# An AdaLN attention and mixture-of-experts block: one-time work between the first batches' operations, written-out orders, and one split f32r product for projection and centred output

## The reference

```python
mod = (silu(c) @ wmod).reshape(16, 6, 1, -1)      # sa, ca, ga, sb, cb, gb
ga, gb = [(2 * (g >= 0) - 1) * maximum(abs(g), 0.25) for g in (ga, gb)]
h = layernorm(x) * (1 + ca) + sa
q, k, v = h @ Wq.T + bq, h @ Wk.T + bk, h @ Wv.T + bv     # 16 heads of 8
q = softmax(q, over the 8 channels of a head); k = softmax(k, over the 512 tokens)
state = k.T @ v                                    # per head, 8 x 8
o = layernorm(q @ state) * ln_g + ln_b
x = x + ga * (o @ Wo.T + bo)
h = layernorm(x) * (1 + cb) + sb
y = sum over the 2 best of 8 experts of p_e * (gelu(h @ w_in[e] + b_in[e]) @ w_out[e] + b_out[e])
x = x + gb * y
```

## Time and profile before

| what | us |
|---|---|
| median of 3 runs | 392.83 (391.58 to 394.48) |
| the profiled execution, its own time | 392.8 |
| its span, first to last instruction | 391.1 |
| PE busy / PEld busy | 362.9 / 327.3 |
| DVE / ACT / POOL busy | 282.5 / 278.5 / 216.8 |
| mean granted TensorE clock | 0.965 |

### The profile page before, as it was taken

One profiled execution on the slowest core, in us unless ns is written; L12 is line 12 of the kernel. 1 busy time (PEld: TensorE's weight loads), 2 busy tenths in 40 slices (PEclk: granted clock), 3 DMA queues, 4 the chain that ended last, 5 costly groups with the idle time before them and its releaser, 6 DMA issues.

```text
span 391.1 us, 8091 instructions
## 1 busy us (share of the span) xinstructions
PE 362.9 (93%) x2502; PEld 327.3 (84%) x2502; DVE 282.5 (72%) x1060; ACT 278.5 (71%) x502; POOL 216.8 (55%) x221
## 2 busy tenths in 40 slices
PE   3657789999999999999999999999999999999995
PEld 3446679889999999899899999898998999988875
DVE  2665586787777888878877778788788787786432
ACT  3333679688787969696887879696969878675740
POOL 2315447373938466483838384664837383754543
PEclk9966579999999999999999999999999999999999
DMA  5570051240706071321606070605224150605061
GB/s 182 151 297 2 0 173 73 80 193 24 247 5 242 29 225 47 157 115 41 231 33 241 3 244 27 240 32 168 106 104 169 38 208 3 217 28 216 32 227 41
DMA packets 18817, 47.83 MB, mean 122 GB/s; under 512 B 2571, under 2 KB 6102, under 8 KB 18518
## 3 DMA queue, kind: packets, MB, share of 16 engines
q1 hardware_dynamic: 18576, 46.90, 33.3%
q10 hardware_dynamic: 198, 0.41, 0.3%
HBM read 42.82 MB, written 4.48 MB: 121 GB/s over the span
## 4 chain that ended last, share of the span: by engine, by line
PE 66%; DVE 9%; issue 6%; DMA 6%; POOL 5%; SPq 4%; ACT 2%; POOLq 0%; DVEq 0%; ACTq 0%
PE pY L684 19%; PE pH L672 6%; PE pH L674 6%; PE pH L673 6%; PE pB L661 4%; PE pQV L641 4%; PE pC L629 4%; PE pC L648 3%; POOL v L355 2%; DVE qn L876 2%; DMA gate_bc<-route_scratch 2%; DMA gates<-gate_scratch 2%; SPq L236 2%; DVE elg_cut L934 2%; PE pA L588 2%
## 5 line engine op out<-in xcount | busy, mean ns | idle before, releaser
L684 PE MATMUL pY<-wout,v 128*128 128x128 f32 x1024 | 128.7, 277 | 1.0 <-DVE v L958 0.7
L684 PEld LDWEIGHTS pY<-wout,v 128*128 128x128 f32 x1024 | 121.7, 193 | 2.2 <-DVE v L958 1.1
L502 ACT ACTIVATE u<-pH,cols 128x512 f32<-128x512 f32 x128 | 86.4, 689 | 49.5 <-PE pH L674 42.8
L344 POOL TENSOR_TENSOR rstd_o<-ve_o,neg_half 128x4 f32<-128x4 f32 x16 | 22.0, 1376 | 104.3 <-DVE ve_o L895 104.3
L958 DVE TENSOR_TENSOR v<-u,gate_bc 128x512 f32<-128x512 f32 x80 | 68.6, 860 | 7.0 <-DMA gate_bc<-route_scratch 3.7
L355 POOL TENSOR_TENSOR v<-u,gate_bc 128x512 f32<-128x512 f32 x48 | 63.7, 1329 | 9.0 <-DMA gate_bc<-route_scratch 9.0
L672 PE MATMUL pH<-h_hi,win_hi 128*128 128x512 f32 x128 | 54.9, 429 | 1.4 <-ACT u L502 1.4
L673 PE MATMUL pH<-h_hi,win_lo 128*128 128x512 f32 x128 | 50.6, 395 | 0.0
L674 PE MATMUL pH<-h_lo,win_hi 128*128 128x512 f32 x128 | 50.5, 394 | 0.0
L349 POOL TENSOR_TENSOR h_lo<-h,h_hi 128x512 fp32r<-128x512 f32 x16 | 22.5, 1405 | 20.2 <-ACT h_hi L440 20.2
L452 ACT ACTIVATE xn<-x_all,nmr,rstd 128x128 f32<-128x128 f32 x64 | 26.2, 482 | 4.5 <-POOL nmr L372 4.5
(11 more groups left out here) (151 smaller groups left out, 781.5 us busy)
## 6 DMA issues: line engine op xcount, KB each, us to landing
gate_bc<-route_scratch SPq DMA_DIRECT2D x64, 512.0 KB, 5.7
x_all<-in_L_attn_x SPq DMA_DIRECT2D x16, 256.0 KB, 6.9
out<-x_all SPq DMA_DIRECT2D x16, 256.0 KB, 2.0
gates<-gate_scratch SPq DMA_DIRECT2D x1, 2048.0 KB, 7.1
gb_bc<-gb_scratch SPq DMA_DIRECT2D x1, 1024.0 KB, 4.6
route_scratch<-gateT SPq DMA_DIRECT2D x64, 4.0 KB
win<-in_L_ffn_w_in SPq DMA_DIRECT2D x1, 512.0 KB, 5.6
wout<-in_L_ffn_w_out SPq DMA_DIRECT2D x1, 512.0 KB, 6.9
```

What stands on the lines that cost most here:

```text
L344: pool.tensor_tensor(rstd_o[:, :], ve_o[:, :], neg_half[:, :], ALU.pow).then_inc(s["rstdo_ready"], 1)
L502: act.activation(u[:, e % U, :], pH[:, e % 2, :], ACT.Gelu_apprx_tanh, bias=cols[:, e:e + 1]).then_inc(s["gelu_done"], 1)
L684: i = mm(pY[:, t * P:(t + 1) * P], v[:, e % U, t * P:(t + 1) * P], wout[:, e, :], start=False, stop=(e == NE - 1), skip_group_check=True)
```

## The change

**One product in place of two.** `attend_centred` and `attend_project` become `attend`: per chunk three f32r matmuls of 256 columns, 12 in all, into `pQV` (before, the projection went to `pC`). `qT` and `sw` become rounded high parts, written by ACT as before, and DVE makes the low parts (`q_low`, `sw_low`). `sq` and `residual1` now read `pQV`, so that `qv(n)` waits for `x1_ready` of batch n - 1, and `state(n)` no longer does.

**One-time work** is cut into functions that stand among the first batches' operations; waits on it move to the operations of batch 0 that use it. The gates are broadcast in two parts, two batches first. Two of the weight loads move to ACT's queue; each load of x signals one of four semaphores.

**Orders.** PE, DVE, ACT, POOL and SP get written-out orders for the first and last batches, and a new `step` between. Cut to its core:

```diff
 PE
-            def attend_centred(n):
-                pe.wait_ge(s["sw_ready"], n + 1)
-                pe.wait_ge(s["qT_ready"], n + 1)
-                for t in range(T):
-                    i = mm(pQT[:, t * P:(t + 1) * P], qT[:, t * P:(t + 1) * P], sw[:, 1, :], start=True, stop=True)
...
+            def attend(n):
+                pe.wait_ge(s["swlow_ready"], n + 1)
+                pe.wait_ge(s["qlow_ready"], n + 1)
+                for t in range(T):
+                    o = pQV[:, t, :, :].rearrange("p a c -> p (a c)")
+                    ts = slice(t * P, (t + 1) * P)
+                    mm(o, qT_hi[:, ts], sw_hi[:, :], start=True, stop=False)
+                    mm(o, qT_hi[:, ts], sw_lo[:, :], start=False, stop=False)
+                    i = mm(o, qT_lo[:, ts], sw_hi[:, :], start=False, stop=True)
+                i.then_inc(s["att_done"], 1)
             def qv(n):
-                w(pe, "sq_ready", n)
+                w(pe, "x1_ready", T * n)
...
+            turn_weights()
+            modulation()
+            hT(0)
+            gain_centred()
+            residual_gates()
+            kT(0)
...
+            gate_turn(15)
+            hidden(14, 6)
+            hidden(14, 7)
+            combine(14, 4)
 DVE
+            def q_low(n):
+                dve.wait_ge(s["qT_ready"], n + 1)
+                w(dve, "att_done", n)
+                dve.tensor_tensor(qT_lo[:, :], pQT, qT_hi[:, :].bitcast(F32), ALU.subtract).then_inc(s["qlow_ready"], 1)
+
+            def sw_low(n):
+                dve.wait_ge(s["sw_ready"], n + 1)
+                w(dve, "att_done", n)
+                dve.scalar_tensor_tensor(out=sw_lo[:, :], in0=pSW, scalar=kinv[:, 0:1], in1=sw_hi[:, :].bitcast(F32),
+                                         op0=ALU.mult, op1=ALU.subtract).then_inc(s["swlow_ready"], 1)
 SP
-                sp.dma_start(gates[:, :, :, :].rearrange("p b w c -> p (b w c)"),
...
+            def spread_first_gates():
+                sp.wait_ge(s["gates_stored"], DMA)
+                sp.dma_start(gates[:, 0:FIRST, :, :].rearrange("p b w c -> p (b w c)"),
```

More of the change, by code:

```diff
@@ L388, in step @@
[L388 to L402 removed]
+                    h_low(b + 4)
@@ L733, in step @@
[L733 to L746 removed]
+                q_turn(b + 2)
+                logits(b + 1)
```

1116 lines of the change are left out of this document (860 added, 256 removed).

## The result

The changed kernel took 401.21 us (median of four runs, 398.88 to 403.47), the kernel before 393.54 beside it: a ratio of 1.0201, 95% interval 1.0122 to 1.028. It is slower by 2%, where 382.8 was forecast and 374.5 to 391 was the range. Its profiled execution took 402.42 us, with a span of 400.7.

The account below looks back on a forecast made before the run. PE's work was taken to fill the loop, 20.93 of 21.44 us a batch, with whole microseconds to gain at start and end. Sum: 392.8 - 4.1 (loop) - 2.2 (start) - 3.7 (end) = 382.8 us; range 374.5 to 391.

Parts of the forecast that it names:

- SP's queue: In the start: the larger part of the gates' broadcast delays only x of batch 3, which nobody needs for 10 us.
- The low parts on DVE: In the loop: q_low 0.69 and sw_low 0.42 us; DVE's busy time from 17.06 to 18.2 us a batch, which fits.
- PE's side of the product: In the loop: 1.42 us for 1.78, with 0.24 given back by f32/f32r changes; PE's work from 20.93 to 20.81.
- The circle: In the loop: from out_var through DVE's work to route and ACT's squares, 20.9 us, as long as PE's work.
- the signs that it named: In the loop: period 21.1 us, out_var's group waiting over 1 us a batch for ACT's squares, attend for no low part.
- the prediction's own signs of being wrong: attend starting late for qT_lo or sw_lo, L958's mean rising beyond 0.95, or the first combine standing after 63 us.
- Twelve periods: Loop between the start and the last batches: 0.34 us saved a period, times 12, 4.1 us; upper bound 7.5.
- The start: First batches: kT(0) at 13.7, gate_turn(0) at 50, first combine at 60.6; 2.2 us saved together, bounds 0 and 7.
- its upper bound: In the start: 7 us saved if PE keeps its full clock.
- The end: Last three batches: 1.5 us of idle time left of 5.2, 3.7 us saved, bounds 1 to 5.
- The rival of slower meetings: In the loop: more DVE operations meet POOL's, 1.1 us a meeting; priced at one and a half a batch, 400 us; chance 0.10.
- the dense loop of 20.9: Loop without PE waits: PE's work 20.81 us; as a rival with a warm start, period 20.85, time 376.7 us, chance 0.20.

Follow-up runs that it names:

- e1: The changed kernel with the loads of x of batches 4 to 10 issued one step earlier in SP's order: 393.37 us, ratio 1.0015.
- e4: e1 with one f32 product of 256 columns in place of the split one, and no low parts: 385.73 us, ratio 0.9779.
- e9: The changed kernel, late loads of x kept, with one f32 product of 256 columns and no low parts: 393.72 us, ratio 1.0019.
- e5: The kernel before with only the loads of x from batch 4 on issued one step later: 524.87 us, ratio 1.3335.
- e11: e1 with both low parts still made by DVE and waited for by PE, but the product in f32 without them: 397.72 us, ratio 1.0107.
- e8: e1 with POOL adding the constant row to one chunk of x of four, a shorter operation: 396.15 us, ratio 1.0069.

## Why the prediction was wrong

**The step that failed: SP's queue.** The prediction says that "the larger part behind it has only x of batch 3 to delay, which nobody needs for 10 us". That came true (batch 3's x led by 15.3 us), but it looked at the start alone, and the sum has no term for the loads of the loop. The new order takes every batch's statistics one step earlier against its load, so that the lead fell from about 18 us to as little as 4.7, where the transfer took 8.8. By e1, e4 and e9 this cost 7 to 9 us in the medians and ratios, and e5, which puts the same order of load and statistics into the kernel before, lost 132 us. It is as large as the measured loss; the other losses and gains of the change cancel (e1, 1.0015).

**The low parts on DVE, priced in the loop alone.** PE's side of the product was sized well: "That is 0.36 saved" and 0.24 given back leave PE's work at 20.81, and in e1 the period of 21.22 less its stop of 0.38 is 20.84. The pieces were off: the product takes 1.51 and not 1.42, and the changes give back less. "The circle is 20.9 us ... so I take a period of 21.1" came true (21.2), with the signs that it named: `out_var` waits 1.10 us a batch for the squares, and `attend` waits for no low part in the loop. Without the low parts the stop is gone and the period is 20.87 (e4), with them and the f32 product it is 21.2 (e11). What the sum lacks is their cost ahead of the loop: of the 9.2 us between the profiled spans of e1 and e4, 5.2 lie in the first six intervals (138.5 us for 133.3). There `attend(2)` does start late for `sw_lo`, by 1.45 us, and `attend(1)` in the start for `qT_lo`, by 0.98, one of the prediction's own signs of being wrong.

**Twelve periods.** "times the 12 periods between the start and the last batches" took the loop's pace for intervals that do not have it. In e1, without late loads, the windows of the first four intervals are
```profile
57.39:150.63 93.24, 87.88 (x627) 78.96 (x625) 84.36 (x272) 75.37 (x130) 59.12 (x53) 1.00 0.37 130
```
and in e4
```profile
56.21:147.32 91.11, 88.88 (x608) 79.73 (x608) 79.94 (x264) 75.28 (x129) 58.36 (x53) 1.00 0.39 136
```
In e1 they take 93.2 us for 4 x 21.1 = 84.4; before, 86.0. PE works 87.9 us in them for 85.3, as work of later batches is pulled ahead (627 instructions for 621, though each batch has four fewer); the last batches have that much less. The rest is idle time, 5.4 us for 0.7: waits for `sw_lo`, `qn`, `yg` and `s2T`. In e4 it is 2.2.

**The start** came out near, by compensation and by its clock: `kT(0)` at 15.85 for 13.7, since the second x landed only at 11.02 and DVE stood before it; the first gates' part landed at 23.69 for "before 20"; `gate_turn(0)` at 49.20 for 50, `combine(0, 0)` at 60.35 for 60.6. The start's stage gives 0.6 us after, 1.7 in e1 and 2.9 in e4, for 2.2, all three with a better clock than the profile before (0.83 to 0.89 for 0.60). At 0.63 and 0.66 the new start is longer than the old one, by 2.8 us in e9 and 1.8 in e11. So at a clock near that of before the new start gave nothing; the sum had put a warmer start only into its upper bound. Whether the new order has a part in the clock is not shown.

**The end** seems right and is not: from batch 14's bias on it is 3.4 us shorter in e1 and e4, for 3.7, but of these 2.7 are work that the new order does ahead of that mark (PE is busy 25.61 us behind it before, 22.93 and 22.92 there). The sum had 3.7 us less of idle time in the last three batches, from 5.2. From batch 13's bias to the span's end PE is idle 6.6 us before, with the 4.5 behind its last matmul, which leaves 2.1 to save from. In e1 and e4 it is 5.6 and 5.5: 1.0 saved. The changed kernel saves none, with waits of 0.39 and 0.54 us for DVE at `moe_bias(15)` and at the combine behind it.

**The rival of slower meetings** got a tenth of the chances, with "only placed anew" against it. DVE's busy time rose by 29.7 us, not by 16 x 1.11 = 17.8. The weighing's mean did not rise, it fell from 860 to 796 ns; the meetings went to operations that I had not counted, because they are small: `echosen`, 192 ns on average before, takes 633, `gateT_r` 408 for 227, the first norm's `ve` 318 for 170. What these meetings cost can't be told from e8.

With the late loads and the low parts taken out, e4 has the dense loop of 20.9 that the working describes. Its span is 9.4 us under that of before, where the sum had 10.0, and that the two agree is in part luck: e4's profiled run is its fastest, at the highest clock (383.46 us at a mean of 0.991; 386.55 at 0.982). The nine intervals of the loop give 4.2, the first four take 5.1 back, and start and last batches together give 10.3, of which 3.5 are work moved into the first four, for the 5.9 forecast.

## What to carry to other kernels

When an order is rewritten, list every transfer's lead in the steady loop, from its issue to its first use, and set it against its landing time: in-order queues shift by whole steps, and one step was worth 2% in the new order and 33% in the old. When two products are merged, look for the consumer that needed only the first half: it now waits for both, and if a chain with 0.17 us to spare hangs on it, 0.94 us more become 0.77 of every batch. Judge each half of a change in the order in which it will run: the merged product cost 13 us in the old order and belonged to the best kernel in the new one. And set stages against each other only between marks with the same work behind them and at the same granted clock: the end seemed 3.4 us shorter and had saved 1.0, and the start was shorter or longer as its clock was.

## What the runs showed of the hardware that was not expected

Some DVE operations that begin inside a POOL one are held until that one ends, down to the smallest. In e1, DVE, then POOL:
```profile
285.79 1.01 DVE L1401 TENSOR_TENSOR echosen<-elg,elg_cut 128x32 f32<-128x32 f32 x1
```
```profile
285.47 1.29 POOL L431 TENSOR_TENSOR h_lo<-h,h_hi 128x512 fp32r<-128x512 f32 x1 [1.48 <-ACT h_hi L572]
```
Both end at 286.8, for an operation of 0.19 us. In e1 nine of the 16 `echosen` met `h_low` so, and each ended 0.04 to 0.05 us behind it. The weighings and subtractions of 512 columns that were held end 0.55 us behind the POOL operation (0.54 in the earlier trace rows). It held for a `tensor_scalar` with one tensor operand too (`ve` above, 0.17 us alone), where I had counted only operations with two. The page "SBUF — State Buffer" of the Trainium skill (Who interferes with whom) says that `tensor_scalar`, copy and cast can take the shared pair of ports too, whoever comes first for the whole instruction; by that rule `ve` and the cast `gateT_r` (408 ns on average here) meet POOL as well, and the trace agrees.

It is not so for every operation with its operands in SBUF. In e1 the statistics (`BATCH_NORM_STATS2`, 128 columns, x64) average 277 ns though 42 of them began inside a POOL operation, and the reduction `qsum` averages 685 ns with 12 of 16 begun so. Nor for every POOL operation: weighings that began inside `rstd_O`, a power of 128x4, kept 0.68 or 0.69 us. And a shorter POOL operation made the kernel slower: e8, by 0.5% against e1's ratio.

An f32 matmul of 256 columns costs more than three f32r ones of the same size, but not much: 1.73 us for four chunks in e4, and 1.51 for the twelve in e1. Two f32 products of 128 columns took 0.89 each, 1.78 together, so that merging them saved TensorE 0.05 us and splitting the merged one 0.22, of which the neighbours took half back.
